# Last tile of a fused attention and expert-mixture kernel: the shared part of the down projection before the last pair, that pair one expert at a time, the rest of down in float32, the output in halves

## The reference

```python
x = x + xattn(layernorm(x), ctx)        # both quantised to fp8 in blocks of 128
y = layernorm(x)                        # 2048 tokens, 512 wide
topk_p, topk_idx = top_k(softmax(y @ w_router), 4)       # 128 experts
basis = silu(y @ w_gate).reshape(T, 8, 256) * (y @ w_up).reshape(T, 8, 256)
mix_sel = mix[topk_idx]                 # mix: each expert's weights over the 8 bases
mixed = einsum('tek,tki->tei', mix_sel, basis)
coeff = topk_w * expert_scale[topk_idx]
out = einsum('teh,te->th', mixed @ w_down, coeff)
shared = silu(y @ shared_w_gate) * (y @ shared_w_up) @ shared_w_down
x = x + out + shared
```

## Time and profile before

| | us |
|---|---|
| median of 3 runs (602.70, 599.99, 602.69) | 602.69 |
| profiled execution | 602.66 |
| its span | 600.9 |

### The profile page before, as it was taken

The page is one execution under the profiler, slowest core; times in us unless marked ns, Lnnn a source line. Parts: engine busy times, 40 slices in busy tenths (PEclk is TensorE's granted clock), DMA queues, the critical chain, the costliest instruction groups (busy, mean ns, idle before and its releaser), DMA issues.

```text
span 600.9 us, 7839 instructions
## 1 busy us (share of the span) xinstructions
PE 538.7 (90%) x2571; PEld 252.6 (42%) x2586; DVE 391.8 (65%) x1122; ACT 238.9 (40%) x339; POOL 203.9 (34%) x242
## 2 busy tenths in 40 slices
PE   0359977799799999999999999999999999999983
PEld 0124433344344444444544444444444444444431
DVE  6977888966866676858475777756665748463211
ACT  4677885232524242342433332343334343323110
POOL 2431040384613135544414134725223141402020
PEclk9999999899999999999999999999999999999997
DMA  8624521111022312112123121121211202020101
GB/s 295 247 87 140 176 88 26 36 28 45 17 54 45 113 36 54 36 30 59 26 54 107 26 63 27 37 52 36 46 42 37 52 27 63 9 53 11 44 0 45
DMA packets 61753, 37.10 MB, mean 62 GB/s; under 512 B 49168, under 2 KB 49680, under 8 KB 61712
## 3 DMA queue, kind: packets, MB, share of 16 engines
q1 hardware_dynamic: 61712, 36.59, 22.3%
HBM read 20.72 MB, written 4.19 MB: 41 GB/s over the span
## 4 chain that ended last, share of the span: by engine, by line
PE 70%; DVE 9%; issue 5%; ACT 2%; POOL 1%; DMA 0%; POOLq 0%; DVEq 0%; SPq 0%; ACTq 0%
PE gate L970 28%; PE up L970 28%; PE even L1000 9%; DVE x L1182 2%; PE odd L952 2%; DVE gate_up L1345 2%; PE odd L892 1%; DVE part L1274 1%; ACT L688 1%; DVE down_lo L1345 1%; DVE ctx_m L1104 1%; DMA hT_hi<-hs_hi 0%; DVE hid L1266 0%; PE up L923 0%; PE turn L867 0%
## 5 line engine op out<-in xcount | busy, mean ns | idle before, releaser
L970 PE MATMUL up<-gate_up,zT_hi 128*128 128x512 f16 x600 | 178.7, 380 | 0.7
L970 PE MATMUL gate<-gate_up,zT_hi 128*128 128x512 f16 x600 | 179.3, 381 | 0.0
L704 ACT ACTIVATE silu<-gate,w_back 128x512 f32<-128x512 f32 x75 | 51.6, 688 | 180.0 <-PE gate L970 179.8
L970 PE MATMUL gate<-gate_up,zT_lo 128*128 128x512 f16 x300 | 114.1, 380 | 0.0
L970 PE MATMUL up<-gate_up,zT_lo 128*128 128x512 f16 x300 | 114.0, 380 | 0.0
L1274 DVE SCALAR_TENSOR_TENSOR part<-up,coef,silu 128x256 f32<-128x256 f32 x128 | 55.9, 478 | 52.8 <-PE up L970 51.0
L559 POOL TENSOR_TENSOR hid<-hid,part 128x256 f32<-128x256 f32 x48 | 34.8, 724 | 155.5 <-DVE part L1274 155.4
L970 PEld LDWEIGHTS gate<-gate_up,zT_hi 128*128 128x128 f16 x600 | 58.8, 100 | 66.5 <-issue 1.6
L970 PEld LDWEIGHTS up<-gate_up,zT_hi 128*128 128x128 f16 x600 | 57.9, 98 | 62.4
L543 POOL TENSOR_TENSOR gain<-var,minus_half 128x1 f32<-128x1 f32 x16 | 9.2, 576 | 133.5 <-DVE neg_mean L1196 133.5
L970 PEld LDWEIGHTS gate<-gate_up,zT_lo 128*128 128x128 f16 x300 | 29.4, 98 | 35.7 <-issue 0.6
(11 more groups left out here) (176 smaller groups left out, 799.6 us busy)
## 6 DMA issues: line engine op xcount, KB each, us to landing
ctx_in<-in_ctx SPq DMA_DIRECT2D x16, 256.0 KB, 3.4
x_in<-in_x SPq DMA_DIRECT2D x16, 256.0 KB, 2.9
out<-y_out SPq DMA_DIRECT2D x16, 256.0 KB, 2.2
stage<-in_L_ffn_w_gate SPq DMA_DIRECT2D x2, 1024.0 KB, 7.5
stage<-in_L_ffn_w_up SPq DMA_DIRECT2D x2, 1024.0 KB, 5.0
stage<-in_L_ffn_shared_w_gate SPq DMA_DIRECT2D x1, 1024.0 KB, 7.8
stage<-in_L_ffn_shared_w_up SPq DMA_DIRECT2D x1, 1024.0 KB, 8.8
ctx_qT<-in_L_ffn_w_up SPq DMA_DIRECT2D x1, 1024.0 KB, 12.1
```

The source lines that it names most:

```text
L704: nc.scalar.activation(silu[:, k % 2, :], gate_ps[k % 2][:], ACT.Silu, scale=w_back[:, n:n + 1] if t else 1.0 / LN_GAIN).then_inc(silu_don ...
L970: mm = nc.tensor.matmul(ps[:], zT[a][:, t % 2, kc, :], wgu[:, n - 1 + i, w, kc, :], start=(m == 0), stop=(m == 3 * KC - 1))
```

## The change

Only the last tile (`LAST`, 15) is written differently, and one transfer is added in tile 4.

- The shared 512 hidden values get a scale of their own (`scale_shared`, `h_hi_shared`, `split_shared`), are turned by transfers of four blocks (`turn_shared`), and their 12 matmuls (`shared_down`) stand between pair 2 and the last pair. The sum is added to the residual in `x2` (`add_shared`).
- The last pair is done one expert at a time (`half_pair`): gate and up with 256 columns, a silu and a product each.
- The mixed hidden values are no longer added by GpSimd at the end, nor split or turned by a transfer: TensorE multiplies the sum of the first six experts and the two last products with the identity in float32, which adds and turns them in PSUM (`turn_sum`). ScalarE and VectorE copy one 128-wide block each to `hT32`, which lies in `y2`.
- Down of these 256 values is done in float32 with unsplit weights (`down_last`), loaded again in tile 4 (`load_down32`) into the stage buffer `stage[0]`, in two halves of 256 output columns, each added (`finish_half`) and stored (`store_last`) by itself.

```diff
+        LAST, HALF = TILES - 1, I
+        hT32 = y2[:, 0:I].rearrange("p (c n) -> p c n", n=P)
+        down32 = stage[0][:, 0:I // P * D].rearrange("p (c w) -> p c w", c=I // P)
...
+            def turn_shared():
+
+                sp.wait_ge(down_full, LAST)
+                sp.wait_ge(h_hi_done, LAST + 1)
+                sp.dma_start_transpose(hT[HI][:, I // P:HC], hs[HI][:, I:HW]).then_inc(hT_in[HI], 16)
+                sp.wait_ge(tail_step, 5)
+                sp.dma_start_transpose(hT[LO][:, I // P:HC], hs[LO][:, I:HW]).then_inc(hT_in[LO], 16)
+
+            def load_down32():
+                wait_ready(sp, 8)
+                wait_first_tile(sp, 8)
+                sp.dma_start(down32, w_down.rearrange("(c p) w -> p c w", p=P)).then_inc(down32_in, 16)
+
+            def store_last(i):
+                sp.wait_ge(tail_done, i + 1)
+                cols = slice(i * HALF, (i + 1) * HALF)
+                sp.dma_start(out_t[LAST * P:, cols], y_out[:, LAST % 2, cols]).then_inc(stored[LAST % 2], 16)
...
-            turn_h(TILES - 1)
-            store(TILES - 1)
+                if t == NB:
+                    load_down32()
+            turn_shared()
+            store_last(0)
+            store_last(1)
...
-            mix_parts(TILES - 1, 3)
...
+            def h_hi_shared():
+                act.wait_ge(tail_step, 4)
+                act.wait_ge(hT_in[HI], 16 * LAST)
+                nc.scalar.activation(hs[0][:, I:HW], hid[:, LAST % 2, I:HW], ACT.Copy, scale=hid_scale[:]
+                                     ).then_inc(h_hi_done, 1)
+
+            def silu_half(i):
+                k, n = use(LAST, PAIRS - 1) + i, chunk(PAIRS - 1)
+                act.wait_ge(gate_full, k + 1)
+                act.wait_ge(up_read, k - 1)
+                nc.scalar.activation(silu[:, k % 2, 0:I], gate_ps[k % 2][:, 0:I], ACT.Silu, scale=w_back[:, n:n + 1]
+                                     ).then_inc(silu_done, 1)
+
+            def keep_h32():
+                act.wait_ge(tail_turned, 1)
+                act.wait_ge(z_lo_done, LAST)
+                nc.scalar.copy(hT32[:, 0, :], turn_ps[0][:, 0:P]).then_inc(tail_kept, 1)
...
-                silus(t, 3)
+                if front:
+                    silus(t, 3)
+                else:
+                    h_hi_shared()
+                    silu_half(0)
                 if front:
                     keep_weight(t + 1)
-            h_hi(TILES - 1)
+            silu_half(1)
+            keep_h32()
...
+            def shared_down():
+                pe.wait_ge(top_step, TOP_STEPS * LAST + 1)
+                n = 0
+                for a, w in HI_LO:
+                    if w == 0:
+                        pe.wait_ge(hT_in[a], 16 * (LAST + 1))
+                    for hc in range(I // P, HC):
+                        mm = nc.tensor.matmul(odd_ps[:], hT[a][:, hc, :], wd[w][:, hc, :],
+                                              start=(n == 0), stop=(n == 3 * (HC - I // P) - 1))
+                        n += 1
+                mm.then_inc(tail_shared_full, 1)
+
+            def half_pair(i):
+
+                k, n = use(LAST, PAIRS - 1) + i, chunk(PAIRS - 1)
+                for j, (ps, full) in enumerate(((gate_ps[k % 2], gate_full), (up_ps[k % 2], up_full))):
+                    m = 0
+                    pe.wait_ge((silu_done, up_read)[j], k - 1)
+                    for kc in range(KC):
+                        for a, w in HI_LO:
+                            mm = nc.tensor.matmul(ps[:, 0:I], zT[a][:, LAST % 2, kc, :],
+                                                  wgu[:, n - 1 + j, w, kc, i * I:(i + 1) * I],
+                                                  start=(m == 0), stop=(m == 3 * KC - 1))
+                            m += 1
+                    mm.then_inc(full, 1)
+
+            def turn_sum(i):
+
+
+                if i == 0:
+                    pe.wait_ge(coef_done, LAST + 1)
+                    pe.wait_ge(mix_acc, MIX_ACC * LAST + 2 * PAIRS - 3)
+                    pe.wait_ge(kept1, turn_of(LO, *TURNS[LO][-1]) + 1)
+                else:
+                    pe.wait_ge(up_read, use(LAST, PAIRS - 1) + i)
+                h = hid[:, LAST % 2, 0:I] if i == 0 else part[:, i - 1, 0:I]
+                for c in range(I // P):
+                    mm = nc.tensor.matmul(turn_ps[c][:, 0:P], h[:, c * P:(c + 1) * P], ident32[:],
+                                          start=(i == 0), stop=(i == 2))
+                if i == 2:
+                    mm.then_inc(tail_turned, 1)
+
+            def down_last(i):
+                cols = slice(i * HALF, (i + 1) * HALF)
+                if i == 0:
+                    pe.wait_ge(down32_in, 16)
+                    pe.wait_ge(down_read, LAST)
+                    pe.wait_ge(tail_kept, 2)
+                ps = (even_ps, gate_ps[(use(LAST, PAIRS - 1) + 1) % 2])[i]
+                for c in range(I // P):
+                    mm = nc.tensor.matmul(ps[:, 0:HALF], hT32[:, c, :], down32[:, c, cols],
+                                          start=(c == 0), stop=(c == I // P - 1))
+                mm.then_inc(tail_full, 1)
...
-                pair(t, 3, third)
-            down(TILES - 1)
+                if front:
+                    pair(t, 3, third)
+            shared_down()
+            half_pair(0)
+            turn_sum(0)
+            half_pair(1)
+            turn_sum(1)
+            turn_sum(2)
+            down_last(0)
+            down_last(1)
...
+            def scale_shared():
+
+                ch = Chain(dve, tail_step, 5, 0)
+                dve.wait_ge(shared_abs, LAST + 1)
+                ch.did(nc.vector.tensor_scalar(shared_top[:], shared_sum[:, LAST % 2:LAST % 2 + 1], SMALLEST, TO_2_14,
+                                               ALU.max, ALU.mult))
+                ch.sync()
+                dve.wait_ge(out_scaled, LAST)
+                ch.did(nc.vector.tensor_scalar(hid_unscale[:].bitcast(U32), shared_top[:].bitcast(U32),
+                                               EXPONENT, None, ALU.bitwise_and))
+                ch.sync()
+                ch.did(nc.vector.reciprocal(hid_scale[:], hid_unscale[:]))
+                ch.did(nc.vector.tensor_tensor(out_scale[:], hid_unscale[:], w_back[:, DOWN:DOWN + 1], ALU.mult))
+                return ch
+
+            def split_shared(ch):
+                dve.wait_ge(h_hi_done, LAST + 1)
+                ch.sync()
+                dve.wait_ge(hT_in[LO], 16 * LAST)
+                ch.did(nc.vector.scalar_tensor_tensor(hs[1][:, I:HW], hid[:, LAST % 2, I:HW], hid_scale[:], hs[0][:, I:HW],
+                                                      ALU.mult, ALU.subtract))
+                ch.end()
+
+            def add_shared():
+                dve.wait_ge(tail_shared_full, 1)
+                dve.wait_ge(tail_step, 5)
+                nc.vector.scalar_tensor_tensor(x2[:, LAST % 3, :], odd_ps[:], out_scale[:], x2[:, LAST % 3, :],
+                                               ALU.mult, ALU.add).then_inc(tail_step, 1)
+
+            def part_half(i):
+
+                k, e = use(LAST, PAIRS - 1) + i, KPC * (PAIRS - 1) + i
+                dve.wait_ge(up_full, k + 1)
+                dve.wait_ge(silu_done, k + 1)
+                dve.wait_ge(mix_acc, MIX_ACC * LAST + 2 * PAIRS - 3)
+                nc.vector.scalar_tensor_tensor(part[:, i, 0:I], up_ps[k % 2][:, 0:I], coef[:, LAST % 2, e:e + 1],
+                                               silu[:, k % 2, 0:I], ALU.mult, ALU.mult).then_inc(up_read, 1)
+
+            def keep_h32():
+                dve.wait_ge(tail_turned, 1)
+                nc.vector.tensor_copy(hT32[:, 1, :], turn_ps[1][:, 0:P]).then_inc(tail_kept, 1)
+
+            def finish_half(i):
+                cols = slice(i * HALF, (i + 1) * HALF)
+                ps = (even_ps, gate_ps[(use(LAST, PAIRS - 1) + 1) % 2])[i]
+                dve.wait_ge(tail_full, i + 1)
+                if i == 0:
+                    dve.wait_ge(tail_step, 6)
+                    dve.wait_ge(stored[LAST % 2], 16 * (LAST // 2))
+                nc.vector.tensor_tensor(y_out[:, LAST % 2, cols], ps[:, 0:HALF], x2[:, LAST % 3, cols], ALU.add
+                                        ).then_inc(tail_done, 1)
...
+                if not front:
+                    shared_chain = scale_shared()
...
-            combine(TILES - 1, 3)
-            split_h(scale_h(TILES - 1), TILES - 1)
-            finish(TILES - 1)
+                if not front:
+                    split_shared(shared_chain)
+            part_half(0)
+            add_shared()
+            part_half(1)
+            keep_h32()
+            finish_half(0)
+            finish_half(1)
```

More of the change, by code:

```diff
@@ L262, in build @@
         out_scaled = sem("out_scaled")
+        down32_in = sem("down32_in")
+        tail_step, tail_turned, tail_kept = sem("tail_step"), sem("tail_turned"), sem("tail_kept")
+        tail_shared_full, tail_full, tail_done = sem("tail_shared_full"), sem("tail_full"), sem("tail_done")
```

(6 more changed lines are left out.)

## The result

| us | before | after |
|---|---|---|
| median of 6 runs each | 602.01 (599.99 to 602.70) | 597.07 (595.49 to 597.71) |
| profiled execution | 602.66 | 597.71 |
| its span | 600.9 | 595.9 |
| mean granted clock | 0.991 | 0.994 |

The ratio is 0.9917, 95% interval 0.9896 to 0.9937: faster by 0.8%, so by more than the 0.5% that can be told.

What follows compares the result with a forecast made beforehand. TensorE, busy 90% of the span, was taken as the bound; 17.1 us lay behind the last pair. Replacing that chain and adding the shared part's waits gave span 597.0, 3.9 us less, and 598.8 us; 8-in-10 range 596.8 to 601.0.

Steps and rivals of the forecast that it cites:

- its low part: Shared part's last four matmuls, on the low half of the split values: start at 582.90 after a wait of 1.17 us.
- first turn: Behind the first half of the last pair: two float32 matmuls of 128 columns on TensorE, taken at 0.5 us.
- The sum: Step-by-step times behind pair 2 in the last tile: span 597.0, 3.9 us less, and 598.8 us.
- The 0.33 of size: Last store: half of 256 KB was estimated to land 0.3 us sooner, giving 598.5.
- The shared part: Between pair 2 and the last pair: 2.59 us of matmuls take 5.33 of TensorE's time, 2.74 coming back.
- the low half ends last: In the shared part: the low half's transfer sets the end; the high half may land up to 1.17 us later free.
- the "dearer" rival: Turns and down in float32: turns at 0.93 add 1.0 us, down at 0.43 a record 1.7; chance 0.12.
- the rival of a drop: Shared part's two waits: the clock drops to half behind them, costing 1.67 us, time 600.5; chance 0.10.
- The slower rival: From 580.00 the low clock level stays to the end, 11.07 us added less 1.17: 608.7; chance 0.03.
- Transfers hidden: Shared part: transfers do not delay TensorE, so it ends at 581.02, not 583.76, time 596.1; chance 0.04.
- At nothing: Edits priced at zero: GpSimd's sums, shared scale, add_shared and the w_down load in tile 4, at most 3.8 us uncovered.

Runs made afterwards that it cites:

- the run that hides them: Changed kernel with the shared part's 12 matmuls behind the first half of the last pair instead of ahead; tail 14.66 us, median 594.09, ratio 0.9861.
- the run with the longer wait: Changed kernel with the high half's transfer held until the low half is split, so TensorE waits once, 4.24 us; tail 21.5 us, 602.2 us.

## Why the prediction was right

Step by step, in us:

| step | predicted | measured |
|---|---|---|
| TensorE done with pair 2 | 578.43 | 578.57 |
| shared part starts; its low part starts | 580.00; 582.90 | 580.13; 582.81 |
| first half starts | 583.76 | 583.68 |
| a half; first turn | 2.63; 0.5 | 2.62; 0.45 |
| last half done | 589.52 | 589.37 |
| down starts | 591.36 | 591.30 |
| issue of the last store | 593.78 | 593.76 |
| end of the span | 597.0 | 595.9 |

**The sum.** Up to the store every step came within 0.15 us, counted from the start of the span. A little of that is luck: counted from the end of pair 2, which came 0.14 later than in the trace of before, the shared part took 5.11 us instead of 5.33 and the last half was done after 10.80 instead of 11.09, while copies and down took 0.13 more. The one term that was mis-sized is "Before, 3.21 us lay between it and the end of the span. I keep them": it measured 2.14. It was read from one store, and the same kernel once more showed 0.73 us less; the median of 2.2 us over 16 such stores would have been the better guide, since that last one landed only after 2.7, and the span ended another 0.5 later. The 0.33 of size agree with the 0.3 that the prediction worked out from the Trainium skill, "DMA: Bandwidth & Descriptors", section "Anatomy of one DMA"; its fixed part of about 2.0 us, given there for another issuing path, does not hold for these stores, as the transfers of the changed kernel (KB each, median us to landing) show 1.7 for 128 KB:

```profile
out<-y_out SPq DMA_DIRECT2D x15, 256.0 KB, 2.2
...
stage<-in_L_ffn_w_down SPq DMA_DIRECT2D x1, 512.0 KB, 4.2
...
out<-y_out SPq DMA_DIRECT2D x2, 128.0 KB, 1.7
```

Nor did the trace agree with that estimate beyond its direction, as the prediction had it: by these two parts the 256 KB and 512 KB that it read at 2.2 and 3.8 us would be an estimated 2.6 and 3.2.

**The shared part.** That it returns nothing where it was put was in the sum (5.33 us of TensorE's time for 2.59 us of work; 5.11 measured) and is now shown by itself: alone it is 1.1 us slower than before, behind the first half 2.5 us cheaper. That the low half ends last is shown too: 0.93 us.

**Float32.** A record of 128 columns takes 0.11 us (0.45 for four), of 256 columns 0.235 (0.94 for four, 591.30 to 592.24; 0.215 predicted), so the "dearer" rival did not come. Its rows ran at half this pace; that this was the lower level, as the prediction read them, fits the factor of two, but the granted clock reads 1.00 over them, so it is not shown.

**The clock.** It stayed at 1.00 through waits of 1.40 and 0.79 us and the burst between, against the rival of a drop. The Trainium skill ("TensorE: Matmul & The Clock Gate", section "HAM oscillation") tells of a kernel whose short bursts of matmuls start cold behind every wait of some 3 to 5 us for a transfer. The trace agrees for the wait of 4.24 us, and shorter waits of 1.40 and 0.79 us, with a burst between, did not lower the clock here. The slower rival, low level to the end, was not seen even behind that wait.

**Transfers hidden.** They were not; the run that hides them shows that this rival would have given 2.5 us, as it was priced (2.7).

**At nothing.** The load of w_down landed after 4.2 us and no wait in tile 5 is put down to it; of the edits, halves of the pair are worth 0.32 us and half stores 0.33 in place of one on the changed kernel, none on before.

## What to carry to other kernels

Work that is moved ahead to fill a gap is worth what its operands allow: look up when they land, and put something that waits for nothing in front of it (2.5 us here). Where values must be added and then turned between engines, multiplying with the identity in float32 can do both on TensorE, and removes maximum, scale, split and transfer from the path (5.4 us here, of which 1.5 because the long wait went and the clock no longer fell). Take the length of a kernel's last transfer from more than one execution before it goes into a sum.

## What was not expected of the hardware

- What a drop of the clock costs hangs on how much of it falls on work. The granted clock stood at 0.50 from 581.3 to 588.2 in the run with the longer wait and from 587.6 to 594.4 in the kernel before, about as long; the wait covered 1.8 us of the one and 3.7 of the other, so 5.1 and 3.1 us of work ran slow. Why it fell 2.6 us after pair 2's end in the one (578.71) and 4.0 after the last pair's end in the other (583.61) stays open.
- The same program differs by 2 us from run to run, and the drops of the granted clock ahead of the last tile do not explain all of it. The six runs of after are 597.71, 597.55 and 597.20 us at a mean clock of 0.994, and 596.93, 595.70 and 595.49 at 0.997. The trace of after has two drops, seen as two digits of 8 on its page. The trace of the pair whole with the shared part under the turns, mean clock 0.997, has one, from 116.4 to 119.8; its page shows none, because that stretch is split between two slices:

```profile
PEclk9999999999999999999999999999999999999999
```

```profile
116.40:119.80 3.40, 3.40 (x10) 1.21 (x9) 2.73 (x7) 0.00 (x0) 0.49 (x1) 0.50 0.00 0
```

With one drop less that trace reaches pair 2's products only 0.32 us sooner than the trace of after (578.44 and 578.76). Why a run has one drop or two, and where the rest of the 2 us comes from, stays open; nothing was tried on it.
